# Attention and grouped normalisation over eight images: one more tile of each middle image in high and low parts, and the squares of y moved from ScalarE to VectorE

## What is computed

```
x_f = Wf x + bf;  x_g = Wg x + bg;  x_h = Wh x + bh
s = x_f^T x_g;  beta = softmax(s, axis=-1)
y = x + gamma * (x_h beta)
nrm = sqrt(sum of y*y over the places), per image and channel
cos = mean over images of (y/nrm)(y/nrm)^T
partners of a channel: itself and 3 more, chosen by the smallest |cos|
mean, var of each channel: over its partners, per image
out = gn_gamma * (y - mean) / sqrt(var + eps) + gn_beta
```

## Time and profile before

| what | value |
|---|---|
| median of 3 runs | 203.44 us (203.13 to 203.77) |
| the profiled execution's own time | 203.12 us |
| its span, first to last instruction | 201.3 us |
| busy share of the span: PE, DVE, ACT, POOL | 89%, 77%, 77%, 59% |
| mean granted TensorE clock over the span | 0.961 |
| split tiles (instructions of L275) | 39 |

### The profile page before, as it was taken

The page is one execution under the profiler, slowest core; times in us unless marked ns, Lnnn a source line. Parts: engine busy times, 40 slices in busy tenths (PEclk is TensorE's granted clock), DMA queues, the critical chain, the costliest instruction groups (busy, mean ns, idle before and its releaser), DMA issues.

```text
span 201.3 us, 2728 instructions
## 1 busy us (share of the span) xinstructions
PE 180.0 (89%) x786; PEld 124.3 (62%) x786; DVE 154.4 (77%) x378; ACT 155.6 (77%) x259; POOL 119.7 (59%) x104
## 2 busy tenths in 40 slices
PE   7889999999999999999999999999999989994000
PEld 2634644587777776787678676867687756663000
DVE  1695868886989788968897889869986996575650
ACT  2376578789999999989998999899999979520420
POOL 4000000928978797979887996799779985620400
PEclk9999999999999999999999999999999999999555
DMA  5990100020002000200011001100020000000298
GB/s 181 328 387 15 40 3 0 2 54 0 0 3 52 0 0 0 55 2 3 0 26 26 3 0 26 26 2 3 2 52 0 0 3 0 0 0 0 100 406 330
DMA packets 4014, 10.72 MB, mean 53 GB/s; under 512 B 544, under 2 KB 672, under 8 KB 4000
## 3 DMA queue, kind: packets, MB, share of 16 engines
q1 hardware_dynamic: 3424, 9.18, 13.6%
q10 hardware_dynamic: 576, 1.38, 1.8%
HBM read 4.52 MB, written 4.19 MB: 43 GB/s over the span
## 4 chain that ended last, share of the span: by engine, by line
PE 79%; DVE 9%; issue 5%; ACT 2%; POOL 1%; DVEq 0%; ACTq 0%; POOLq 0%
PE o_ps L669 43%; PE s_ps L647 13%; PE w_ps L633 6%; PE w_ps L628 6%; PE w_ps L684 3%; PE w_ps L678 3%; DVE nmax L425 2%; PE o_ps L625 2%; DVE xy L618 2%; PE o_ps L770 1%; ACT probs_high L346 1%; DVE values L455 1%; ACT probs L337 1%; DVE g_rows L444 1%; PE s_ps L678 1%
## 5 line engine op out<-in xcount | busy, mean ns | idle before, releaser
L275 POOL TENSOR_TENSOR probs_low<-probs,probs_high 128x1024 fp32r<-128x1024 f32 x39 | 93.2, 2391 | 56.2 <-ACT probs_high L346 56.2
L425 DVE TENSOR_REDUCE nmax<-s_ps 128x1 f32<-128x1024 f32 x64 | 77.7, 1217 | 10.6 <-PE s_ps L647 10.6
L337 ACT ACTIVATE probs<-s_ps,nmax 128x1024 f32<-128x1024 f32 x64 | 71.1, 1111 | 17.1 <-DVE nmax L425 17.1
L647 PE MATMUL s_ps<-g_rows,fg_parts 128*128 128x512 f32 x128 | 47.5, 455 | 1.4 <-ACT probs L337 0.7
L669 PE MATMUL o_ps<-probs,vnorm 128*128 128x512 f32 x100 | 47.0, 592 | 0.0
L346 ACT ACTIVATE probs_high<-probs 128x1024 fp32r<-128x1024 f32 x39 | 41.0, 1051 | 0.1
L669 PE MATMUL o_ps<-probs_high,v_high 128*128 128x512 f32 x78 | 34.0, 436 | 0.7 <-POOL v_low L297 0.7
L669 PE MATMUL o_ps<-probs_low,v_high 128*128 128x512 f32 x78 | 30.6, 392 | 0.0
L669 PE MATMUL o_ps<-probs_high,v_low 128*128 128x512 f32 x78 | 30.6, 392 | 0.0
L647 PEld LDWEIGHTS s_ps<-g_rows,fg_parts 128*128 128x128 f32 x128 | 21.4, 190 | 11.6 <-issue 6.8
L669 PEld LDWEIGHTS o_ps<-probs,vnorm 128*128 128x128 f32 x100 | 18.7, 189 | 14.9 <-issue 12.7
(11 more groups left out here) (87 smaller groups left out, 174.8 us busy)
## 6 DMA issues: line engine op xcount, KB each, us to landing
xy<-x_dram SPq DMA_DIRECT2D x7, 512.0 KB, 5.7
out_dram<-xy SPq DMA_DIRECT2D x5, 512.0 KB, 5.9
g_rows<-fg_parts SPq DMA_DIRECT2D x14, 128.0 KB, 2.2
out_dram<-xy ACTq DMA_DIRECT2D x2, 512.0 KB, 4.3
xy<-x_dram SPq DMA_DIRECT2D x2, 256.0 KB, 3.9
out_dram<-xy SPq DMA_DIRECT2D x2, 256.0 KB, 2.7
wd<-wide_dram ACTq DMA_DIRECT2D x1, 256.0 KB, 4.5
wd<-wide_dram ACTq DMA_DIRECT2D x1, 66.5 KB, 3.7
```

Of the source, the lines that this page charges most:

```text
L275: nc.gpsimd.tensor_tensor(probs_low[i % PARTS][:, :], probs[n % PROBS][:, :], probs_high[i % PARTS][:, :].bitcast(F32), ALU.subtract).then ...
L337: nc.scalar.activation(probs[n % PROBS][:, :], s_ps[n % 2][:, :], ACT.Exp, bias=nmax[:, n % T:n % T + 1], accum_out=rsum[:, n % T:n % T + ...
L425: nc.vector.reduce_max(nmax[:, n % T:n % T + 1], s_ps[n % 2][:, :], AX_X, negate=True).then_inc(max_ready, 1)
L647: last = nc.tensor.matmul(s_ps[n % 2][:, h], fg_parts[b % 2][:, t * P:(t + 1) * P], g_rows[b % 2][:, h], start=True, stop=True)
```

## The change

The whole tile of each middle image is now only t = 6, where before it was t = 1 and t = 4; so seven of eight tiles are split in place of six, five more over the kernel. The squares of the y of images 0 to 6 leave ScalarE's stream and go into VectorE's, in the same slot t = 2: behind the bias of the values and ahead of the row maximum. There they are one scalar_tensor_tensor, (y times 1) times y with the row sum, from SBUF into SBUF.

```diff
-WHOLE_LATER = (1, 4)
+WHOLE_LATER = (6,)
...
                         negate_high(b + 1, 1)
-                    if t == 2 and b > 0:
-                        act.wait_ge(y_ready, H * b)
-                        nc.scalar.activation(squares[:, :], xy[:, b - 1, :], ACT.Square,
-                                             accum_out=stats[:, b - 1 + B:b + B]).then_inc(sq_ready, 1)
                     if t == 4 and b > 0:
...
                         add_value_bias(1, t - 3, w_ps)
+                    if t == 2 and b > 0:
+                        dve.wait_ge(y_ready, H * b)
+                        nc.vector.scalar_tensor_tensor(squares[:, :], xy[:, b - 1, :], 1.0, xy[:, b - 1, :], ALU.mult,
+                                                       ALU.mult, accum_out=stats[:, b - 1 + B:b + B]).then_inc(sq_ready, 1)
                     if t == 5 and b > 0:
                         dve.wait_ge(yT_high, b)
```

## The result

The changed kernel takes 214.42 us (median of 4 runs, 214.08 to 214.6) where the kernel before, run beside it, takes 203.61: a ratio of 1.0537, 95% interval 1.0519 to 1.0555. It is slower, as forecast; the forecast of 209.5 us was too low by 4.9 (a rise of 10.8 us for one of 6.4), and the rival in which the square and GpSimd take turns, 215.3, is the nearer. The span grew from 201.3 to 212.4 us. Each time here is a median of several executions; one execution of the kernel with tile 4 whole and two operands took 379.58 us, where its others took some 217, and is left out of its median.

The account below looks back on a forecast made before the run. TensorE bounds the kernel before; afterwards GpSimd's order would set the middle images' period. Entry 2.36, images 3 to 6 4.04, exit -0.75 and +0.76 give +6.4 us on 203.12: 209.5 us, range 205.5 to 216.8.

Parts of the forecast that it names:

- What bounds the kernel, and the gain forgone: TensorE sets the middle images' pace, 20.99 us; splitting a tile saves it 0.34 us, 1.7 us over five images.
- Order: Middle images: GpSimd's tiles 3, 4, `invert_norm`, 5 make TensorE wait 1.35 us ahead of tile 5; period 22.00 us.
- The square beside GpSimd: VectorE's square and GpSimd's subtraction, both reading two SBUF operands, were taken not to hold each other up: nothing added.
- the add in the tail: Small VectorE add of two SBUF operands, 0.15 us beside GpSimd's power; taken as evidence that the square costs no waiting.
- the first rival: Square waits for GpSimd's subtraction, then holds GpSimd 1.15 us, in five images: 215.3 us, or 216.4 with image 7's; chance 0.33.
- VectorE's queue at no cost: Middle images: work queued behind VectorE's squares, the bias late by some 0.56 us, was costed at nothing.
- Worse: VectorE's late bias also holds transposes and tile 6's scores, another 0.56 us an image on top of turns: over 217; chance 0.04.
- Entry and exit: Entry, image 1 to image 2's tile 5: +2.36 us; exit, image 6's tile 5 into image 7: -0.75 and +0.76.
- TensorE keeps the pace: Rival: GpSimd's 20.40 us fit into TensorE's 20.65 and high parts come early enough: 201.4 us; chance 0.10.
- a draw: Rival: a remaining stall of 0.34 us an image eats the gain: 203.1 us; chance 0.05.

Follow-up runs that it names:

- tile 4 whole and two operands: The changed kernel with tile 4 alone whole in place of tile 6 alone, squares on VectorE with two SBUF operands: 216.94 us, ratio 1.0656.
- The list alone: The kernel before with only its whole tiles changed, to tile 6 alone; squares stay with ScalarE: 208.70 us, ratio 1.0238.
- the one-operand run: The changed kernel with VectorE's instruction on y summing the larger of y and 1, from one SBUF operand: 209.59 us, ratio 1.0287.
- On the old list the same move: The kernel before, tiles 1 and 4 whole, with the instruction on y moved to VectorE with one SBUF operand: 207.79 us, ratio 1.0195.

## Why the prediction was right in sign and too low in size

- *What bounds the kernel, and the gain forgone.* Right. TensorE's 0.34 us per tile was never collected, since the image no longer ran at TensorE's pace.
- *Order.* Right. The list alone gave a period of 22.03 us for the 22.00 of the chain, a wait of 1.29 for 1.35, and 208.70 us; with an instruction of VectorE's that has one operand, the loop agrees in each link, and the time is 209.59 us for the 209.5 of the sum. That this fits to 0.1 us is in part luck: against the kernel before run beside it (203.81) the rise is 5.8 us for 6.4. One reading in the argument was off, though not in the sum: TensorE makes tile 4's scores 7.2 us after the tile 5 of the image before (112.97 to 120.13 in the kernel before), not some 13.
- *The square beside GpSimd: "I take nothing".* This is the step that failed. I took the low end of a bound from the add in the tail, which was not held up by a power. That row has one element per partition, and why it was not held up no run shows; the squares on 1024 are held up by the subtraction they meet, by just what is left of it (1.29, 1.84 us), and hold GpSimd's low values up by 1.0. The term, put at nothing in the sum and measured at 0.95 us an image and 4.8 in all, is the first rival's; it had put 1.15 and 5.75, as the square's whole work, where GpSimd loses 1.0 of it. The time lies in the stated range only because the range took in this rival, given 0.33; the forecast's own 207 to 212, given 0.48, missed it.
- *The rule of the Trainium skill.* "SBUF — State Buffer", section "Who interferes with whom", says that a VectorE instruction with two SBUF inputs and a GpSimd instruction that reads SBUF exclude each other for the whole of the first one. The changed kernel's trace agrees: 2.42 us against 1.22 with GpSimd idle, 1.45 against 0.46; and so does the one-operand run, 1.21 us throughout. I had let one small row outweigh it.
- *VectorE's queue at no cost.* Right for the changed kernel (0.02 us an image net of what ScalarE is spared, read with one operand), but the reason I gave, that GpSimd doesn't ask for tile 6, is not the whole of it: the copy of the turned y and the gram stand behind the same queue, and there the pair that tile 6 no longer needs and TensorE's own wait for tile 5 make the room. On the old list the same move cost 0.74 us an image (21.73 less 20.99), in part through the gram, which I hadn't named. The late bias of "Worse" shows as a gap of 0.11 us ahead of the transposes (to 115.79 in image 4).
- *Entry and exit.* The entry was +3.5 for 2.36; the square of image 2 met a subtraction there (2.97 us). The list alone came in at 74.13, +1.7, where the sum without the square's delay gives 2.36 - 0.84 = 1.52. Of the exit's two terms neither came: from image 6's tile 5 to image 7's tile 0 TensorE takes 7.78 us (166.42 to 174.20), not 7.06, as it waits there for VectorE's residual of image 6, which the sum had left out; and no wait of 0.76 us stands ahead of image 7's tile 2. That -0.75 and +0.76 cancel is luck. PE of the changed kernel at image 7's tile 0:

```profile
174.20 0.47 PE L669 MATMUL o_ps<-probs_high,v_high 128*128 128x512 f32 x1 [0.56 <-DVE xy L456]
```

- *"TensorE keeps the pace" and "a draw".* Both shut out: 7 x 2.79 + 0.87 fit into an image as a load, and the list alone still lost 5 us.

## What to carry to other kernels

That an engine's work fits into a period says nothing of whether it fits between two others' instructions: take one loop from a wait of the bound engine back to itself, in the order of the streams, and add it up. When work is moved to another engine, look at what stands behind it in that queue, two engines further on as well. And if it is to run beside GpSimd, count the SBUF operands: here an instruction of the same size at the same place cost 4.8 us more with two than with one.

## What the runs showed that I had not expected

VectorE's square (128x1024, both operands from SBUF) waits for GpSimd's running subtraction to end, to 0.01 us (1.29 and 1.84 us, each plus 1.13 of its own), and then keeps the next GpSimd instruction for 1.0 us; in both timelines the wait is hidden in a longer instruction, not shown as idle time. Once GpSimd's low values went first instead. DVE and POOL with tile 4 whole and two operands, image 2:

```profile
64.57 3.39 DVE L514 SCALAR_TENSOR_TENSOR squares<-xy 128x1024 f32<-128x1024 f32 x1
...
66.38 0.50 POOL L297 TENSOR_TENSOR v_low<-vnorm,v_high 128x128 fp32r<-128x128 f32 x1
```

There the low values took their usual time, and the square, 3.39 us, waited for both. What decides who goes first no run shows. And moving ScalarE's squares by a single slot, with GpSimd's power, cost 3.9 us (204.21 to 208.08), by a copy two instructions behind it.
